# Moving one low-part subtraction ahead of the layer-norm block in GpSimd's loop (gated cross-attention block, one Trainium2 core)

## The chip, the cores and the metric

The kernel runs on one core of one Trainium2 chip. The metric is the device time of one execution in microseconds. Three executions of the kernel before took 1097.84, 1102.97 and 1105.66 us; the median is 1102.97 us.

## The reference, cut to what matters

x and ctx are 128 batches of 128 rows by 256 columns in float32; there are 16 heads of 16 columns. The mask is one 128 by 128 pattern for all batches.

```python
def reference(x, ctx, mask, g_xattn, g_ffn, Wv, bv, Wk, bk, Wq, bq, Wo, bo, W1, W2, W3, b):
    q = layernorm(x) @ Wq + bq
    k, v = ctx @ Wk + bk, ctx @ Wv + bv
    energy = einsum('nqhd,nkhd->nhqk', q, k)        # by head
    energy = where(mask == 0, finfo.min, energy)
    attn = softmax(energy / sqrt(16))
    x = x + tanh(g_xattn) * (einsum('nhqk,nkhd->nqhd', attn, v) @ Wo + bo)
    h = layernorm(x) @ W1 @ W2 @ W3
    return x + tanh(g_ffn) * tanh(h + b)
```

## The kernel before, in words

The 128 batches are taken in pairs: `NP` is 64 pairs, and every engine has a loop over `t` from 0 to 63 with its own order written out by hand. Nothing schedules the work but this order and semaphores. Several stages of different pairs are in flight in one iteration: scores and softmax of pair t, projections of pair t+1, the layer norm of x of pair t+2, the transport of the attention result of pair t-2, its division and output projection for pairs t-3 and t-4, the second layer norm of pair t-4, and the feed-forward part of pairs t-5 and t-6. One iteration is called a period here.

Float32 products of full accuracy are made from two parts: a tile is split into a high part (ScalarE copies it into the float32r type, line 748) and a low part (the tile less its high part: line 958 on VectorE, lines 414 and 425 on GpSimd). A projection (`project`, line 503, `project_T`, line 496) then takes 12 matmuls.

The attention result of a pair, `a_den`, leaves as sums and denominators. SyncE writes it to DRAM (`write_a`, line 263), reads the denominators (`read_den`, 271), writes their reciprocals (`write_reciprocals`, 253), reads the sums in another layout (`read_a`, 277: `a_rows`) and reads the reciprocals spread over the rows (`read_wide`, 258: `den_wide`). GpSimd multiplies both (`divide_a`, line 420: `a_norm`) once both have landed. ScalarE makes the high part of `aT` (`high_of_a`, line 748), GpSimd the low part (`low_of_a`, line 425, which waits for `aT_high` and for the output projection of the pair before). TensorE's output projection of that pair (`make_o`, line 503) comes in the next period. VectorE adds the residual (`add_residual`, 1015) and makes the moments of the second layer norm (`moments_of_y`, 1022 and 1026).

In a period GpSimd works in this order (lines 449 to 473): `low_of_ctx` (414), `add_ffn_bias` (431), `divide_a` (420), `finish` (436), `add_out_bias` (410), a wait for the moments of x of pair t+2 and of y of pair t-4, `rstd` (lines 369 to 383, eight small operations for both), `normalise_x` (389: `xn`), `normalise_y` (389: `yn`), `low_of_a` (425).

TensorE transposes `xn` in `turn_x` (line 490), which waits for `xn_ready` and for `k_ready`: the transposes go to the bank that held the k projection, and ScalarE has to have copied it out (`spread_k`, 773). ScalarE's loop puts `high_of_a` ahead of `spread_q` (773), a softmax exponent (798), `keep_a` (805), `high_of_y` (748) and `spread_k`.

SyncE issues all DMAs of the loop in one order (lines 309 to 332). Its relevant part is `write_reciprocals`, `read_a`, `write_y` (293: `yn` to DRAM, waits for `yn_ready`), `read_max` (288: the row maxima into `q_aug`, for the transposed scores on line 624), `read_wide` (258), then of the next period `store` (305) and `read_y` (299: waits until the write of `yn` has landed), `write_max` (281), `read_den`, `read_max`, `write_a`, the loads of x (202) and ctx (211), `write_max`, and so on to the next `read_a`.

Of the kernel before, what the change touches and what calls it, by code (L numbers as in the profile page):

```python
# [30 lines left out]
def gated_xattn_block(nc, x, ctx, mask, g_xattn, g_ffn, Wv, bv, Wk, bk, Wq, bq, Wo, bo,  # L31
# [9 lines left out]
    with ExitStack() as stack:  # L41
# [123 lines left out]
        def wait(eng, semaphore, value):  # L165
            if value > 0:
                eng.wait_ge(semaphore, value)

        def is_pair(p):
            return 0 <= p < NP  # L170
# [14 lines left out]
        def flat(a):  # L185
            return a.rearrange("p a b -> p (a b)")
# [169 lines left out]
        def _(pool):  # L356
# [7 lines left out]
            def rstd(run):  # L364

                vp, r, a, b, nm = (ln_t[:, j, :] for j in range(5))
                moments = stat2[run % 2][:].rearrange("p a b z -> p (a b) z")
                mean, var = moments[:, :, 0], moments[:, :, 1]
                nc.gpsimd.tensor_tensor(vp, var, c_eps[:], ALU.add).then_inc(ln_step, 1)
                pool.wait_ge(ln_step, RSTD * run + 1)  # L370
                nc.gpsimd.tensor_tensor(r, vp, c_minus_half[:], ALU.pow).then_inc(ln_step, 1)
                pool.wait_ge(ln_step, RSTD * run + 2)
                nc.gpsimd.tensor_tensor(a, r, r, ALU.mult).then_inc(ln_step, 1)
                pool.wait_ge(ln_step, RSTD * run + 3)
                nc.gpsimd.tensor_tensor(b, a, vp, ALU.mult).then_inc(ln_step, 1)
                pool.wait_ge(ln_step, RSTD * run + 4)
                nc.gpsimd.tensor_scalar(a, b, -0.5, 1.5, ALU.mult, ALU.add).then_inc(ln_step, 1)
                pool.wait_ge(ln_step, RSTD * run + 5)
                nc.gpsimd.tensor_tensor(r, r, a, ALU.mult).then_inc(ln_step, 1)
                pool.wait_ge(ln_step, RSTD * run + 6)  # L380
                nc.gpsimd.tensor_tensor(a, mean, r, ALU.mult).then_inc(ln_step, 1)
                pool.wait_ge(ln_step, RSTD * run + 7)
                nc.gpsimd.tensor_scalar(nm, a, -1.0, None, ALU.mult).then_inc(ln_step, 1)  # L383
                pool.wait_ge(ln_step, RSTD * run + 8)
# [7 lines left out]
            def normalise_x(p):  # L392
                wait(pool, xT_done, p)
                pool.wait_ge(x_landed[p % X_RING], 16 * (p // X_RING + 1))
                normalise(0, xn, x_in[p % X_RING], xn_ready)

            def normalise_y(p):
                if p <= END + 1:
                    wait(pool, yn_stored, 16 * p)
                else:  # L400
                    pool.wait_ge(yT_done, p - 1 - END)
                pool.wait_ge(y_ready, p + 1)
                normalise(1, yn, y[p % Y_RING], yn_ready)

            def add_out_bias(p):
                if p == 0:
                    pool.wait_ge(bo_ready, 1)
                pool.wait_ge(xn_ready, PAIR * (p + 1))
                tile = x_in[p % X_RING][:]
                nc.gpsimd.tensor_tensor(tile, tile, bo_wide[:].unsqueeze(1).to_broadcast([P, PAIR, E]), ALU.add).then_inc(x_biased, 1)  # L410

            def low_of_ctx(p):
                pool.wait_ge(cT_high, p + 1)
                nc.gpsimd.tensor_tensor(flat(cT[:, 1]), flat(ctx_T[:]), flat(cT[:, 0]), ALU.subtract).then_inc(cT_ready, 1)

            def divide_a(p):
                pool.wait_ge(a_landed, 16 * (p + 1))
                pool.wait_ge(wide_landed, 16 * (p + 1))
                wait(pool, aT_ready, p)
                nc.gpsimd.tensor_tensor(a_norm[:], a_rows[:], den_wide[:], ALU.mult).then_inc(a_norm_ready, 1)  # L420

            def low_of_a(p):
                pool.wait_ge(aT_high, p + 1)
                wait(pool, o_done, p)
                nc.gpsimd.tensor_tensor(flat(aT[:, 1]), a_norm[:], flat(aT[:, 0]), ALU.subtract).then_inc(aT_ready, 1)

            def add_ffn_bias(p):
                if p == 0:
                    pool.wait_ge(bf_landed, 16)
                pool.wait_ge(f_kept, p + 1)  # L430
                nc.gpsimd.tensor_tensor(th[:], th[:], bf_wide[:].unsqueeze(1).to_broadcast([P, PAIR, E]), ALU.add).then_inc(f_biased, 1)

            def finish(p):
                pool.wait_ge(th_gated, p + 1)
                tile = flat(y[p % Y_RING][:])
                nc.gpsimd.tensor_tensor(tile, tile, flat(th[:]), ALU.add).then_inc(res_ready, 1)
# [12 lines left out]
            for t in range(NP):  # L449
                if t > 0 and is_pair(t + 1):  # L450
                    low_of_ctx(t + 1)
                if is_pair(t - 6):
                    add_ffn_bias(t - 6)
                if is_pair(t - 3):
                    divide_a(t - 3)
                if is_pair(t - 6):
                    finish(t - 6)
                if is_pair(t - 2):
                    add_out_bias(t - 2)
                if t == NP - 1:  # L460
                    add_out_bias(t - 1)
                    add_out_bias(t)
                if is_pair(t + 2):
                    pool.wait_ge(stat1_ready, t + 3)
                if is_pair(t - 4):
                    pool.wait_ge(stat2_ready, t - 3)
                rstd(t + 2)
                if is_pair(t + 2):
                    normalise_x(t + 2)
                if is_pair(t - 4):  # L470
                    normalise_y(t - 4)
                if is_pair(t - 3):
                    low_of_a(t - 3)
            for p in range(NP - 4, NP - 1):
                pool.wait_ge(stat2_ready, p + 1)
                rstd(p + 6)
# [723 lines left out]
```

## Time and profile before

| what | value |
|---|---|
| median of three executions | 1102.97 us (1097.84 to 1105.66) |
| the profiled execution | 1105.66 us |
| its span, first to last instruction | 1103.9 us |
| outside the span | 1.8 us |
| mean granted TensorE clock | 0.987 |
| TensorE busy | 1038.0 us, 94% |
| VectorE busy | 954.7 us, 86% |
| ScalarE busy | 831.2 us, 75% |
| GpSimd busy | 798.3 us, 72% |

The profile gives the busy time of each engine as a share of the span. An engine that is idle is not thereby harmless: it can be idle because it waits in a circle with others. A matmul's end is modelled, so that TensorE's busy time shows only roughly how full it is.

### The profile page before, as it was taken

What the parts mean: (1) busy time and instruction counts of PE and PEld (TensorE: products, weight loads), DVE (VectorE), ACT (ScalarE), POOL (GpSimd) and SP (SyncE); (2) the same over time, 40 slices, a digit from 0 to 9 for tenths busy, and PEclk for the clock granted to TensorE, in tenths of its full rate; (3) what the DMA queues carried; (4) which work ended last, traced back from release to release, by engine and by line L of the source; (5) the groups of instructions that cost most, each with busy time, mean ns of one, the idle gap of its engine ahead of it and who ended that gap; (6) DMA issues with size and microseconds to landing.
All of it is one profiled execution on the core that took longest, in us unless ns stands there. A gap on an engine that the chain in (4) does not pass through costs nothing.

```text
span 1103.9 us, 45278 instructions
## 1 busy us (share of the span) xinstructions
PE 1038.0 (94%) x18487; PEld 897.8 (81%) x18487; DVE 954.7 (86%) x1331; ACT 831.2 (75%) x1275; POOL 798.3 (72%) x1184
## 2 busy tenths in 40 slices
PE   5888999999999999999999999999999999989965
PEld 5777888888888888888888888888788888878855
DVE  5778899889889989889998998999898898888866
ACT  4465878888788787777878878787787877878742
POOL 5254777787787778777778777877777877777653
PEclk9899999999999999999999999999999999999988
DMA  5133555555555564555555556555555555554432
GB/s 150 44 101 104 153 149 159 158 146 155 152 155 155 140 172 139 160 155 146 163 147 154 156 144 168 152 156 149 151 156 145 161 149 154 159 140 138 126 124 68
DMA packets 260400, 158.87 MB, mean 144 GB/s; under 512 B 174945, under 2 KB 227170, under 8 KB 260194
## 3 DMA queue, kind: packets, MB, share of 16 engines
q1 hardware_dynamic: 260050, 155.72, 50.8%
q8 instruction: 147, 2.41, 0.9%
q14 instruction: 59, 0.48, 0.2%
q10 hardware_dynamic: 144, 0.26, 0.1%
HBM read 85.92 MB, written 68.94 MB: 140 GB/s over the span
## 4 chain that ended last, share of the span: by engine, by line
PE 26%; POOL 18%; issue 16%; DMA 15%; SPq 13%; DVE 6%; ACT 6%; POOLq 0%; DVEq 0%; ACTq 0%
PE ps_m L503 6%; DMA a_rows<-scratch_a 5%; PE ps_m L496 5%; PE ps_s L603 4%; PE ps_x L635 3%; DMA scratch_y<-yn 3%; DMA den_wide<-scratch_r 3%; ACT k_aug L773 3%; POOL a_norm L420 3%; SPq L211 3%; SPq L288 3%; POOL yn L389 3%; DVE probs L1007 3%; SPq L299 3%; PE ps_s L624 3%
## 5 line engine op out<-in xcount | busy, mean ns | idle before, releaser
L996 DVE TENSOR_REDUCE neg_max<-ps_s 128x16 f32<-128x2048 f32 x128 | 293.1, 2290 | 68.7 <-PE ps_s L609 68.7
L1007 DVE TENSOR_TENSOR probs<-ps_s,far_T 128x2048 f32<-128x2048 f32 x128 | 291.2, 2275 | 26.3 <-PE ps_s L624 25.5
L798 ACT ACTIVATE probs<-probs 128x2048 f32<-128x2048 f32 x128 | 244.5, 1910 | 5.6 <-DVE probs L1007 5.5
L420 POOL TENSOR_TENSOR a_norm<-a_rows,den_wide 128x512 f32<-128x512 f32 x61 | 78.6, 1288 | 173.6 <-issue 171.6
L603 PE MATMUL ps_s<-k_aug,q_aug 32*128 32x128 f32 x4096 | 150.2, 282 | 17.7 <-DVE probs L1007 7.5
L624 PE MATMUL ps_s<-q_aug,k_aug 32*128 32x128 f32 x4096 | 153.0, 285 | 7.4 <-DMA q_aug<-scratch_m 4.3
L603 PEld LDWEIGHTS ps_s<-k_aug,q_aug 32*128 32x128 f32 x4096 | 127.8, 186 | 38.3 <-issue 30.8
L624 PEld LDWEIGHTS ps_s<-q_aug,k_aug 32*128 32x128 f32 x4096 | 128.7, 188 | 25.4 <-DMA q_aug<-scratch_m 5.8
L635 PE MATMUL ps_x<-probs,v_ones 128*32 128x128 f32 x4096 | 141.2, 279 | 3.9 <-issue 3.1
L773 ACT ACTIVATE q_aug<-ps_m,q_bias,q_scale 128x256 f32<-128x256 f32 x256 | 122.8, 559 | 17.3 <-PE ps_m L496 9.0
L635 PEld LDWEIGHTS ps_x<-probs,v_ones 128*32 128x32 f32 x4096 | 106.1, 111 | 33.5 <-issue 33.4
L773 ACT ACTIVATE k_aug<-ps_m,k_bias,parity 128x256 f32<-128x256 f32 x256 | 123.7, 569 | 11.6 <-PE ps_m L496 10.8
L748 ACT ACTIVATE aT<-a_norm 128x512 fp32r<-128x512 f32 x64 | 40.5, 632 | 114.6 <-POOL a_norm L420 106.1
L565 PE MATMUL ps_m<-wv_s,cT 128*128 128x256 f32 x756 | 118.5, 293 | 0.0
L503 PE MATMUL ps_m<-wo_s,aT 128*128 128x256 f32 x768 | 110.8, 294 | 4.3 <-DVE aT L958 3.1
L496 PE MATMUL ps_m<-cT,wk_s 128*128 128x256 f32 x768 | 109.1, 292 | 3.4 <-DVE wk_s L929 2.0
L503 PEld LDWEIGHTS ps_m<-wo_s,aT 128*128 128x128 f32 x768 | 97.3, 192 | 17.8 <-issue 17.2
L503 PE MATMUL ps_m<-wf_s,yT 128*128 128x256 f32 x756 | 107.1, 292 | 2.8 <-DVE yT L958 2.7
L496 PEld LDWEIGHTS ps_m<-cT,wk_s 128*128 128x128 f32 x768 | 96.1, 190 | 15.9 <-issue 13.2
L496 PE MATMUL ps_m<-xT,wq_s 128*128 128x256 f32 x768 | 108.1, 290 | 0.3 <-DVE xT L958 0.3
L565 PEld LDWEIGHTS ps_m<-wv_s,cT 128*128 128x128 f32 x756 | 99.2, 190 | 8.5 <-issue 1.0
L389 POOL TENSOR_SCALAR xn<-x_in,ln_t 128x256 f32<-128x256 f32 x128 | 97.4, 766 | 6.8 <-POOL ln_t L383 0.2
(123 smaller groups left out, 1769.2 us busy)
## 6 DMA issues: line engine op xcount, KB each, us to landing
scratch_a<-a_den SPq DMA_DIRECT2D x64, 512.0 KB, 3.3
x_in<-in_x SPq DMA_DIRECT2D x64, 256.0 KB, 4.4
a_rows<-scratch_a SPq DMA_DIRECT2D x64, 256.0 KB
den_wide<-scratch_r SPq DMA_DIRECT2D x64, 256.0 KB
out<-y SPq DMA_DIRECT2D x64, 256.0 KB, 4.6
ctx_in<-in_ctx SPq DMA_DIRECT2D x252, 64.0 KB, 2.9
scratch_y<-yn SPq DMA_DIRECT2D x59, 256.0 KB, 3.8
y_blocks<-scratch_y SPq DMA_DIRECT2D x236, 64.0 KB
```

The lines of the kernel that those rows point to most:

```text
L389: nc.gpsimd.tensor_scalar(dst[:, i, :], src[:, i, :], ln_t[:, 1, j:j + 1], ln_t[:, 4, j:j + 1], ALU.mult, ALU.add).then_inc(ready, 1)
L420: nc.gpsimd.tensor_tensor(a_norm[:], a_rows[:], den_wide[:], ALU.mult).then_inc(a_norm_ready, 1)
L496: last = nc.tensor.matmul(dst[:, m * TOK:(m + 1) * TOK], w[:, a, k, m * P:(m + 1) * P], src[:, b, k, :], start=(n == 0), stop=(n == len(TE ...
L503: last = nc.tensor.matmul(dst[:, i * E:(i + 1) * E], src[:, a, k, i * P:(i + 1) * P], w[:, b, k, :], start=(n == 0), stop=(n == len(TERMS) ...
L565: last = nc.tensor.matmul(dst[:, i * E:(i + 1) * E], cT[:, a, k, i * P:(i + 1) * P], wv_s[:, b, k, :], start=(n == 0), stop=(n == len(TERM ...
L603: nc.tensor.matmul(ps_s[:, j, s, :], q_aug[p % 2][rows, n, s, :], k_aug[p % 2][rows, n, s, :], start=(s == 0), stop=False, tile_position=( ...
L624: last = nc.tensor.matmul(ps_s[:, j, s, :], k_aug[p % 2][rows, n, s, :], q_aug[p % 2][rows, n, s, :], start=True, stop=True, tile_position ...
L635: last = nc.tensor.matmul(ps_x[j * ROWS:(j + 1) * ROWS, s, :], v_ones[p % V_RING][:, n, h, :], probs[i % 2][:, j, s, :], start=True, stop= ...
L773: last = nc.scalar.activation(dst[:, :, 2 * m + a, :], src[:, m * TOK:(m + 1) * TOK].rearrange("p (n q) -> p n q", q=P), ACT.Identity, bia ...
L798: nc.scalar.activation(tile, tile, ACT.Exp).then_inc(probs_ready, 1)
L996: nc.vector.tensor_reduce(neg_max[:, 0:H].rearrange("p (j c) -> p j c", j=G), ps_s[:], AX.X, ALU.max, negate=True).then_inc(max_ready, 1)
L1007: nc.vector.tensor_tensor(probs[i % 2][:].rearrange("p j s q -> p (j s) q"), ps_s[:].rearrange("p j s q -> p (j s) q"), far_T[:].unsqueeze ...
```

## The change

On GpSimd, in every period, `low_of_a(t - 3)` is issued after `add_out_bias` and before the wait for the moments, `rstd`, `normalise_x` and `normalise_y`; before, it was the last operation of the period. Its own waits and operands stay as they are. No instruction is added or taken away, and the other engines' orders, SyncE's DMA order among them, are the same.

```diff
@@ -460,6 +460,8 @@
                 if t == NP - 1:
                     add_out_bias(t - 1)
                     add_out_bias(t)
+                if is_pair(t - 3):
+                    low_of_a(t - 3)
                 if is_pair(t + 2):
                     pool.wait_ge(stat1_ready, t + 3)
                 if is_pair(t - 4):
@@ -469,8 +471,6 @@
                     normalise_x(t + 2)
                 if is_pair(t - 4):
                     normalise_y(t - 4)
-                if is_pair(t - 3):
-                    low_of_a(t - 3)
```

GpSimd's order in the middle of a period, before, from the bias on the residual input to the low part of `aT`:

```order
L410 TENSOR_TENSOR x_in<-x_in,bo_wide 128x512
L369 TENSOR_TENSOR ln_t<-stat,c_eps 128x4
L371 TENSOR_TENSOR ln_t<-ln_t,c_minus_half 128x4
L373 TENSOR_TENSOR ln_t<-ln_t 128x4
L375 TENSOR_TENSOR ln_t<-ln_t 128x4
L377 TENSOR_SCALAR ln_t<-ln_t 128x4
L379 TENSOR_TENSOR ln_t<-ln_t 128x4
L381 TENSOR_TENSOR ln_t<-stat,ln_t 128x4
L383 TENSOR_SCALAR ln_t<-ln_t 128x4
L389 TENSOR_SCALAR xn<-x_in,ln_t 128x256 x2
L389 TENSOR_SCALAR yn<-y,ln_t 128x256 x2
L425 TENSOR_TENSOR aT<-a_norm,aT 128x512
```

The same place after the change:

```order
L410 TENSOR_TENSOR x_in<-x_in,bo_wide 128x512
L425 TENSOR_TENSOR aT<-a_norm,aT 128x512
L369 TENSOR_TENSOR ln_t<-stat,c_eps 128x4
L371 TENSOR_TENSOR ln_t<-ln_t,c_minus_half 128x4
L373 TENSOR_TENSOR ln_t<-ln_t 128x4
L375 TENSOR_TENSOR ln_t<-ln_t 128x4
L377 TENSOR_SCALAR ln_t<-ln_t 128x4
L379 TENSOR_TENSOR ln_t<-ln_t 128x4
L381 TENSOR_TENSOR ln_t<-stat,ln_t 128x4
L383 TENSOR_SCALAR ln_t<-ln_t 128x4
L389 TENSOR_SCALAR xn<-x_in,ln_t 128x256 x2
L389 TENSOR_SCALAR yn<-y,ln_t 128x256 x2
```

The subtraction on line 425 now stands ahead of the ten operations that lead to `xn` and `yn`, and these come one operation later; what follows them (line 414, then 431 and 420) directly follows `yn`.

The last iteration, t = 63, which has no `xn` and three biases in a row (line 410, x3), before:

```order
L420 TENSOR_TENSOR a_norm<-a_rows,den_wide 128x512
L436 TENSOR_TENSOR y<-y,th 128x512
L410 TENSOR_TENSOR x_in<-x_in,bo_wide 128x512 x3
L369 TENSOR_TENSOR ln_t<-stat,c_eps 128x4
L371 TENSOR_TENSOR ln_t<-ln_t,c_minus_half 128x4
L373 TENSOR_TENSOR ln_t<-ln_t 128x4
L375 TENSOR_TENSOR ln_t<-ln_t 128x4
L377 TENSOR_SCALAR ln_t<-ln_t 128x4
L379 TENSOR_TENSOR ln_t<-ln_t 128x4
L381 TENSOR_TENSOR ln_t<-stat,ln_t 128x4
L389 TENSOR_SCALAR yn<-y,ln_t 128x256 x2
L425 TENSOR_TENSOR aT<-a_norm,aT 128x512
```

Here too the row of line 425 moves up to stand directly behind the three biases. Pairs 61 to 63 have their low part made on VectorE, which the change does not touch.

## Rows read from the trace of the kernel before

**Rows 1.** The page: busy time and share of the span.
```profile
PE 1038.0 (94%) x18487; PEld 897.8 (81%) x18487; DVE 954.7 (86%) x1331; ACT 831.2 (75%) x1275; POOL 798.3 (72%) x1184
```

**Rows 2.** The page: the chain that ended last, by engine.
```profile
PE 26%; POOL 18%; issue 16%; DMA 15%; SPq 13%; DVE 6%; ACT 6%; POOLq 0%; DVEq 0%; ACTq 0%
```

**Rows 3.** Timeline of TensorE, transposes of xn: start, duration, what [idle before <-releaser].
```profile
504.85 0.66 PE L490 MATMUL ps_m<-ident,xn 128*128 128x128 f32 x4
521.68 0.66 PE L490 MATMUL ps_m<-ident,xn 128*128 128x128 f32 x4 [0.57 <-ACT k_aug L773]
537.71 0.66 PE L490 MATMUL ps_m<-ident,xn 128*128 128x128 f32 x4
```

**Rows 4.** Line 420 alone: duration min/median/max, first and last start.
```profile
L420 POOL TENSOR_TENSOR a_norm<-a_rows,den_wide x61: 1267/1289/1299, 73.8 to 1050.1; 128x512 f32<-128x512 f32 x61
```

**Rows 5.** Timeline of GpSimd over one period.
```profile
513.17 1.29 POOL L420 TENSOR_TENSOR a_norm<-a_rows,den_wide 128x512 f32<-128x512 f32 x1 [3.87 <-issue]
...
516.90 0.20 POOL L369 TENSOR_TENSOR ln_t<-stat,c_eps 128x4 f32<-128x4 f32 x1
...
520.05 1.45 POOL L389 TENSOR_SCALAR xn<-x_in,ln_t 128x256 f32<-128x256 f32 x2
521.49 1.09 POOL L389 TENSOR_SCALAR yn<-y,ln_t 128x256 f32<-128x256 f32 x2
522.54 1.29 POOL L425 TENSOR_TENSOR aT<-a_norm,aT 128x512 fp32r<-128x512 f32 x1
523.78 1.28 POOL L414 TENSOR_TENSOR cT<-ctx_T,cT 128x512 fp32r<-128x512 f32 x1
525.01 1.28 POOL L431 TENSOR_TENSOR th<-th,bf_wide 128x512 f32<-128x512 f32 x1
528.36 1.29 POOL L420 TENSOR_TENSOR a_norm<-a_rows,den_wide 128x512 f32<-128x512 f32 x1 [2.06 <-issue]
```

**Rows 6.** Timeline of SyncE's queue, the two places around read_a.
```profile
506.04 0.41 SPq L293 DMA_DIRECT2D scratch_y<-yn  x1
...
521.26 0.61 SPq L277 DMA_DIRECT2D a_rows<-scratch_a  x1
522.60 0.38 SPq L293 DMA_DIRECT2D scratch_y<-yn  x1
523.03 1.09 SPq L288 DMA_DIRECT2D q_aug<-scratch_m  x2
524.23 0.61 SPq L258 DMA_DIRECT2D den_wide<-scratch_r  x1
```

**Rows 7.** Waits of the whole run: us in total, times, longest.
```profile
POOL a_norm L420 <- issue: 171.6, 60, 5.4
...
POOL ln_t L369 <- DVE stat L1026: 19.8, 16, 7.3
...
SPq L293 <- POOL yn L389: 36.3, 46, 2.5
```

**Rows 8.** Timeline of SyncE's queue: read_wide in two other periods.
```profile
588.34 0.61 SPq L258 DMA_DIRECT2D den_wide<-scratch_r  x1
...
928.42 0.61 SPq L258 DMA_DIRECT2D den_wide<-scratch_r  x1
```

**Rows 9.** Timeline of GpSimd in those periods and the one after.
```profile
585.60 1.09 POOL L389 TENSOR_SCALAR yn<-y,ln_t 128x256 f32<-128x256 f32 x2
592.34 1.27 POOL L420 TENSOR_TENSOR a_norm<-a_rows,den_wide 128x512 f32<-128x512 f32 x1 [1.93 <-issue]
597.48 0.20 POOL L369 TENSOR_TENSOR ln_t<-stat,c_eps 128x4 f32<-128x4 f32 x1 [1.37 <-DVE stat L1026]
602.30 1.08 POOL L389 TENSOR_SCALAR yn<-y,ln_t 128x256 f32<-128x256 f32 x2
609.92 1.29 POOL L420 TENSOR_TENSOR a_norm<-a_rows,den_wide 128x512 f32<-128x512 f32 x1 [2.73 <-issue]
...
933.65 1.30 POOL L420 TENSOR_TENSOR a_norm<-a_rows,den_wide 128x512 f32<-128x512 f32 x1 [3.17 <-issue]
```

**Rows 10.** Timeline of VectorE: the low part of yT.
```profile
519.84 0.69 DVE L958 TENSOR_TENSOR yT<-y_T,yT 128x512 fp32r<-128x512 f32 x1 [0.38 <-ACT yT L748]
```

**Rows 11.** Timelines at the end of the loop: GpSimd, then TensorE.
```profile
1060.78 1.27 POOL L425 TENSOR_TENSOR aT<-a_norm,aT 128x512 fp32r<-128x512 f32 x1
...
1064.88 1.70 PE L503 MATMUL ps_m<-wo_s,aT 128*128 128x256 f32 x12 [0.34 <-DVE th L1049]
```

## The prediction

> **What bounds the kernel now.** I read the page first. Its busy shares [rows 1] show TensorE at 94% and GpSimd at 72%, so at first sight an order on GpSimd cannot matter. The chain that ended last says otherwise [rows 2]: TensorE holds only 26% of it, GpSimd 18%, DMA 15%, SyncE's queue 13%, and 16% is time that nothing in the profile explains. A chain through four engines that repeats is a circle, so I looked for its round time.
>
> The timeline of TensorE gives one side. Its transposes of xn start at 504.85, 521.68 and 537.71 [rows 3]: 16.83 us with 0.57 us of idle time, then 16.03 us with none shown. So TensorE alone could do a period in about 16.04 us. The real mean comes from line 420, whose 61 executions start from 73.8 to 1050.1 [rows 4]: 976.3/60 = 16.27 us. TensorE loses some 0.2 us a period, always at turn_x.
>
> The timeline of GpSimd gives the other side. From the start of a_norm (513.17) to the end of yn (521.49+1.09 = 522.58) are 9.41 us without a gap [rows 5]. I call it the GpSimd leg. From there to the next a_norm (528.36) are 5.78 us, the return leg. In it SyncE sends yn out at 522.60, 0.02 us after it is ready, then the maxima, then den_wide at 524.23, which is issued at 524.84 [rows 6]; a_norm starts 3.52 us after that. GpSimd's own work in the return leg ends at 526.29 and it waits 2.06 us [rows 5]. Over the run it waits 171.6 us in 60 waits ahead of a_norm, 2.86 us each, and SyncE waits for yn in 46 periods [rows 7]. So in most periods this holds: a_norm, yn, SyncE's write_y, read_wide, landing, a_norm. GpSimd's idle time is not slack, it is the return leg of a circle that passes through GpSimd itself. The mean return leg is the 3.71 us of work (522.58 to 526.29) and 2.86 us of waiting, 6.57 us, which leaves 16.27-6.57 = 9.70 us for the GpSimd leg: 9.41 and some waits for the moments (19.8 us in 16 waits [rows 7]) and for a longer xn. The circle closes in the same 16.27 us as TensorE's period. Both are bounds within a quarter of a microsecond.
>
> **The change, part by part.** low_of_a leaves the return leg and enters the GpSimd leg. Its price is the distance between starts, 522.54 to 523.78, 1.24 us [rows 5].
>
> In the return leg it was covered: GpSimd waited 2.06 us (mean 2.86) behind it, and what ends the wait is a landing and not GpSimd. Taking it out saves nothing; the wait becomes 1.24 us longer.
>
> In the GpSimd leg it is not covered in full periods: 9.41+1.24 = 10.65 us. Only where GpSimd waits for the moments does it fill that wait, in 16 periods of about 60. It brings no wait of its own: ScalarE's high part is made as soon as a_norm is there, 1.3 us after its start, and low_of_a would come 3.73 us after it (516.90 [rows 5]). Behind it stand rstd, xn and yn. turn_x started 0.18 us after the end of xn at 521.68 (520.05+1.45 = 521.50 [rows 3, 5]), so TensorE gets xn up to 1.1 us late, and SyncE sends yn, the maxima and den_wide 1.24 us late.
>
> What is gained by the early aT is nothing: TensorE reads it a period later. In the last iteration the low part ends at 1062.05 and the projection starts at 1064.88, released by a bias on VectorE [rows 11], so the end gains nothing either.
>
> The return leg after the change is the unknown. It is 0.02 us, then 1.63 us from write_y to the issue of den_wide, 0.61 us for that issue [rows 6] (2.26 us together), and the landing. The landing depends on what shares the DMA engines, most of all a_rows, issued just ahead of yn. If yn comes later, a_rows has had more of them to itself. The nearest rows are the 16 of 55 periods in which den_wide was issued at least 2.6 us behind the end of read_a's issue. Their landings run from 3.39 us (588.95 to 592.34) to 4.62 us (929.03 to 933.65) [rows 8, 9], with a mean of 3.91. The new return leg is then 2.26+3.9, about 6.15 us, and between 5.65 and 6.9. The new period is 10.65+6.15 = 16.8 us, with 16.3 and 17.5 as ends.
>
> A second circle checks this. From write_y (506.04) over all of SyncE's period to the end of read_a's issue (521.87) are 15.83 us, and from there 6.49 us to a_norm (528.36) [rows 5, 6]; with the new GpSimd leg two periods take 15.83+6.49+10.65 = 32.97, 16.5 us each. I take the middle of 16.5 and 16.8 with a little more weight on the direct sum, 16.75. Against 16.27 that is 0.5 us for each of the 57 steps from t=4 to t=61 in which the circle exists: 28 us. Below nothing is possible only down to TensorE's 16.04, since no circle can be quicker than it.
>
> The sum: the profiled execution has 1103.9 us of span and 1.8 us around it, 1105.7; with 28 us it would take 1134. The median is 2.7 us below that execution, so the median forecast is 1103+28 = 1131 us.
>
> **A rule beside a row.** The pair of xn took 1.45 us and the equal pair of yn 1.09 [rows 5]. VectorE's subtraction for yT ran from 519.84 to 520.53, across the start of xn at 520.05 [rows 10]. The Trainium skill (SBUF — State Buffer, "SBUF: two separate sides") says that VectorE, in an operation with two SBUF inputs, and GpSimd lock one shared pair of ports against each other for a whole instruction. By that rule the trace agrees, and xn, which moves 1.24 us later, would miss that operation. But VectorE's subtraction then falls on the small operations of rstd, which read SBUF too. I count no gain; the rule's other outcome is the second rival.
>
> **The rivals.**
>
> First, the later issue is paid back by the landing. With den_wide landing at the shortest row, 3.39 us, in all periods, the return leg is 5.65 us and the period 16.3; some periods still hide low_of_a in the wait for the moments. The cost is then 0.03 to 0.15 us a period, about 6 us: 1109. For it speaks that a late issue has short landings (3.52 and 3.39 in rows 6 and 9); against it that 4.62 stands in the same group. The Trainium skill (DMA: Bandwidth & Descriptors, "Latency and other measured facts") says that a lighter memory load makes the fixed part of a DMA smaller, which would help this rival; no row here separates that part.
>
> Second, the change is faster. xn gets rid of the collision with yT's subtraction (0.36 us, 1.45 less 1.09), and rstd doesn't pick it up. The GpSimd leg is 10.29 us, and with 5.65 the circle closes in 15.94 us, less than TensorE's 16.04. Then TensorE never waits and the period is 16.04: 57 times 0.23 is 13 us less, 1090. It decides only if both hold, and the shortest of 55 landings would have to be the rule. Very unlikely.
>
> Third, it is worse than forecast. When yn was late in the kernel before, the return leg did not shorten. In the period with a_norm at 592.34 GpSimd waited 1.37 us for the moments, yn ended at 603.38, and the next a_norm came at 609.92, 6.54 us later [rows 9]. A return leg of 6.45 with 10.65 is 17.1 us, 0.85 more than now: 48 us, 1151. For it speaks that SyncE's later reads (yn's blocks, the maxima of both halves) shift as well, and TensorE can wait for maxima where it waited for xn. Against it: that period's a_norm had come early, so part of the distance is TensorE's own time.
>
> **How the numbers follow.** The forecast, 1131 with 1117 to 1145 around it, has 0.66. The first rival (1109) has 0.17, the second (1090) 0.05, the third (1151) 0.12. A difference under about 1%, 11 us, can't be told from none in this kernel. Slower by over 1% is the forecast and the third rival, 0.78; within 1% is the first, 0.17; faster is the second, 0.05. The range takes in the first rival and the third and leaves out the second: 1106 to 1152.
>
> **What would show it.** In the trace after, a_norm's starts should lie 16.75 us apart on average. From a_norm to the end of yn should be 10.6 to 10.7 us, and waits for the moments rare. turn_x should start 0.18 us or less after the end of xn in nearly every period, with TensorE idle some 0.6 us ahead of it. SyncE should wait longer ahead of write_y than 36.3/46 = 0.8 us, and the wait ahead of a_norm should be more than 2.86 us. ScalarE's wait for a_norm should not be what TensorE then waits for. If a_norm's distance stays at 16.3 with a GpSimd leg of 10.65, the first rival was right, and den_wide's landing shows it; if the leg itself is under 10.4, the collision is gone. The prediction is wrong if TensorE's idle time doesn't grow at turn_x, or if another operation than a_norm, yn or xn is what it waits for.

## The result, and the profile after

The changed kernel takes 1151.9 us (median of four executions, 1150.81 to 1156.32 us) against 1103.03 us for the kernel before. The ratio is 1.0446, with a 95% interval of 1.0416 to 1.0478: 4.5% slower, 49 us. The profiled execution has a span of 1145.9 us, 42.0 us more than the 1103.9 us of before. The profiled execution of before was the slowest of its kernel (1105.66 us, 2.6 us above the median), that of the changed kernel the fastest of its (1147.69 us, 4.2 us below the median); so the profiles show 42 us and the medians 49.

The page of the changed kernel, busy shares and the chain that ended last, by engine:

```profile
PE 1032.0 (90%) x18487; PEld 894.1 (78%) x18487; DVE 954.2 (83%) x1331; ACT 831.6 (73%) x1275; POOL 797.5 (70%) x1184
...
POOL 42%; issue 27%; DMA 10%; SPq 9%; PE 7%; DVE 5%; POOLq 0%; ACT 0%; DVEq 0%
```

No engine has more to do than in [rows 1] (ScalarE's 0.4 us more is nothing in 831). What changed is the chain: TensorE's share of it fell from 26% in [rows 2] to 7%, and GpSimd's rose from 18% to 42%, at a busy share of 70%. That fits a circle through GpSimd that closes in every period.

Line 420 alone (duration min/median/max, first and last start):

```profile
L420 POOL TENSOR_TENSOR a_norm<-a_rows,den_wide x61: 1267/1289/1301, 73.8 to 1089.4; 128x512 f32<-128x512 f32 x61
```

The mean distance is (1089.4-73.8)/60 = 16.93 us, where [rows 4] gave 16.27. The 60 steps account for 39.3 of the 42.0 us.

The timeline of GpSimd over a full period of the changed kernel (start, duration, what; idle time before it and its releaser in brackets), the rows that answer to [rows 5]:

```profile
512.94 1.29 POOL L420 TENSOR_TENSOR a_norm<-a_rows,den_wide 128x512 f32<-128x512 f32 x1 [2.72 <-issue]
...
516.68 1.28 POOL L425 TENSOR_TENSOR aT<-a_norm,aT 128x512 fp32r<-128x512 f32 x1
517.93 0.19 POOL L369 TENSOR_TENSOR ln_t<-stat,c_eps 128x4 f32<-128x4 f32 x1
518.20 1.04 POOL L371 TENSOR_TENSOR ln_t<-ln_t,c_minus_half 128x4 f32<-128x4 f32 x1
519.32 0.20 POOL L373 TENSOR_TENSOR ln_t<-ln_t 128x4 f32<-128x4 f32 x1
519.60 0.20 POOL L375 TENSOR_TENSOR ln_t<-ln_t 128x4 f32<-128x4 f32 x1
519.89 0.73 POOL L377 TENSOR_SCALAR ln_t<-ln_t 128x4 f32<-128x4 f32 x1
...
521.61 1.09 POOL L389 TENSOR_SCALAR xn<-x_in,ln_t 128x256 f32<-128x256 f32 x2
522.68 1.09 POOL L389 TENSOR_SCALAR yn<-y,ln_t 128x256 f32<-128x256 f32 x2
524.77 1.28 POOL L414 TENSOR_TENSOR cT<-ctx_T,cT 128x512 fp32r<-128x512 f32 x1 [1.00 <-ACT cT L748]
526.00 1.29 POOL L431 TENSOR_TENSOR th<-th,bf_wide 128x512 f32<-128x512 f32 x1
529.80 1.29 POOL L420 TENSOR_TENSOR a_norm<-a_rows,den_wide 128x512 f32<-128x512 f32 x1 [2.50 <-issue]
```

The leg from a_norm to the end of yn is 523.77-512.94 = 10.83 us here, and the return leg 529.80-523.77 = 6.03 us, together 16.86. GpSimd now waits twice in the return leg, for the high part of cT (1.00 us) and for the landing (2.50 us). Both lie in the shadow of SyncE's path: GpSimd could do more work there, but the leg would not get shorter with less. The same place in SyncE's queue and on TensorE:

```profile
521.44 0.61 SPq L277 DMA_DIRECT2D a_rows<-scratch_a  x1
523.80 0.38 SPq L293 DMA_DIRECT2D scratch_y<-yn  x1
524.23 1.09 SPq L288 DMA_DIRECT2D q_aug<-scratch_m  x2
525.42 0.60 SPq L258 DMA_DIRECT2D den_wide<-scratch_r  x1
```

```profile
522.85 0.63 PE L490 MATMUL ps_m<-ident,xn 128*128 128x128 f32 x4 [1.18 <-POOL xn L389]
539.63 0.63 PE L490 MATMUL ps_m<-ident,xn 128*128 128x128 f32 x4 [0.90 <-POOL xn L389]
```

write_y leaves 0.03 us behind yn, den_wide is issued at 526.02, and a_norm starts 3.78 us later. TensorE starts its transposes 0.15 us behind the end of xn (522.70) and stood idle for 1.18 and 0.90 us; in [rows 3] that was 0.57 us and nothing.

The waits of the whole run (us in total, times, longest):

```profile
POOL a_norm L420 <- issue: 163.6, 60, 3.8
...
POOL cT L414 <- ACT cT L748: 85.2, 62, 11.8
...
PE ps_m L490 <- POOL xn L389: 62.8, 58, 1.5
...
SPq L293 <- POOL yn L389: 96.4, 59, 2.4
```

SyncE waits for yn in all 59 periods in which there is a write_y, 1.63 us each, where [rows 7] had 46 waits of 0.8 us. TensorE waits for xn 58 times, 1.08 us each.

The whole run can be split in the same way. Each period in which there is a write_y runs from one a_norm to the next; the trace has 59 of them. In microseconds:

| mean of 59 periods | before | forecast | after |
|---|---|---|---|
| GpSimd leg, a_norm to the end of yn | 9.65 | 10.65 | 10.73 |
| return leg, end of yn to the next a_norm | 6.63 | 6.15 | 6.24 |
| period | 16.29 | 16.80, taken as 16.75 | 16.98 |

write_y leaves within 0.1 us of the end of yn in 50 of these periods before and in all 59 after. The landing marks in the trace (the semaphore updates of each DMA) show which transfer GpSimd waits for: in both kernels a_norm starts 0.12 to 0.41 us after the last mark of den_wide, and never less than 2.2 us after the last mark of a_rows.

### The profile page after: what moved, and what is told of

Same layout as the page of the kernel before. It is cut to its first block, busy times and chain, and to the rows that moved or that the text cites. A ratio compares the mean times of both kernels' runs of the same rounds, so it can differ in the third digit from the quotient of the medians.

```text
span 1145.9 us, 45278 instructions
## 1 busy us (share of the span) xinstructions
PE 1032.0 (90%) x18487; PEld 894.1 (78%) x18487; DVE 954.2 (83%) x1331; ACT 831.6 (73%) x1275; POOL 797.5 (70%) x1184
## 3 DMA queue, kind: packets, MB, share of 16 engines
q8 instruction: 147, 2.41, 0.9%
## 4 chain that ended last, share of the span: by engine, by line
POOL 42%; issue 27%; DMA 10%; SPq 9%; PE 7%; DVE 5%; POOLq 0%; ACT 0%; DVEq 0%
DMA den_wide<-scratch_r 9%; POOL y L436 6%; POOL xn L389 5%; POOL aT L425 5%; POOL yn L389 5%; POOL ln_t L371 5%; SPq L288 5%; POOL x_in L410 5%; POOL ln_t L377 3%; SPq L293 2%; DVE probs L1007 2%; POOL ln_t L379 2%; DVE neg_max L996 2%; PE ps_s L603 1%; PE ps_s L624 1%
## 5 line engine op out<-in xcount | busy, mean ns | idle before, releaser
L996 DVE TENSOR_REDUCE neg_max<-ps_s 128x16 f32<-128x2048 f32 x128 | 293.2, 2291 | 71.2 <-PE ps_s L609 71.2
L420 POOL TENSOR_TENSOR a_norm<-a_rows,den_wide 128x512 f32<-128x512 f32 x61 | 78.6, 1289 | 167.1 <-issue 163.6
L635 PE MATMUL ps_x<-probs,v_ones 128*32 128x128 f32 x4096 | 138.9, 276 | 2.8 <-issue 2.0
L414 POOL TENSOR_TENSOR cT<-ctx_T,cT 128x512 fp32r<-128x512 f32 x62 | 79.1, 1276 | 85.2 <-ACT cT L748 85.2
L748 ACT ACTIVATE xT<-ps_m 128x512 fp32r<-128x512 f32 x65 | 38.9, 598 | 105.9 <-PE ps_m L490 103.3
```

What stands on the lines that cost most here:

```text
L635: last = nc.tensor.matmul(ps_x[j * ROWS:(j + 1) * ROWS, s, :], v_ones[p % V_RING][:, n, h, :], probs[i % 2][:, j, s, :], start=True, stop= ...
L748: nc.scalar.activation(flat(dst[:, 0]), src, ACT.Copy).then_inc(ready, 1)
L996: nc.vector.tensor_reduce(neg_max[:, 0:H].rearrange("p (j c) -> p j c", j=G), ps_s[:], AX.X, ALU.max, negate=True).then_inc(max_ready, 1)
```

## The experiments

Each ran beside the kernel before on the same chip; the median of the latter was 1099.31 us for the first four, 1098.08 us for the next four and 1097.73 us for the last two. Ratios are against that, in the order of the text. The period is the mean distance of a_norm's 61 starts. Its first and last start are given with each.

**Which of the two late tiles costs: xn or yn.** The low part stands between them, so xn is on time and yn is not.

```diff
                 if is_pair(t + 2):
                     normalise_x(t + 2)
+                if is_pair(t - 3):
+                    low_of_a(t - 3)
                 if is_pair(t - 4):
                     normalise_y(t - 4)
-                if is_pair(t - 3):
-                    low_of_a(t - 3)
```

> The subtraction of line 425 stands between xn and yn: xn is as early after a_norm as before, only yn is 1.24 us later. Circle theory (a_norm, yn, SyncE's write_y and read_wide, landing, a_norm sets the period): the leg from a_norm to the end of yn is 10.65 to 10.75 us, the return 6.2, period 16.9 to 17.0, about 1145 to 1152 us like the changed kernel, and TensorE no longer waits for xn but for k_aug. Rival, that TensorE gets xn late and this alone costs: 1103 us as before. A time between (about 1125) would mean that both count.

It took 1143.21 us, ratio 1.0405 (1.037 to 1.0439). The period is (1084.8-71.4)/60 = 16.89 us, against 16.93 in the changed kernel. GpSimd and TensorE in one of its periods:

```profile
512.11 1.29 POOL L420 TENSOR_TENSOR a_norm<-a_rows,den_wide 128x512 f32<-128x512 f32 x1 [3.95 <-issue]
...
519.00 1.45 POOL L389 TENSOR_SCALAR xn<-x_in,ln_t 128x256 f32<-128x256 f32 x2
520.42 1.29 POOL L425 TENSOR_TENSOR aT<-a_norm,aT 128x512 fp32r<-128x512 f32 x1
521.69 1.10 POOL L389 TENSOR_SCALAR yn<-y,ln_t 128x256 f32<-128x256 f32 x2
529.20 1.28 POOL L420 TENSOR_TENSOR a_norm<-a_rows,den_wide 128x512 f32<-128x512 f32 x1 [3.93 <-issue]
```

```profile
520.63 0.65 PE L490 MATMUL ps_m<-ident,xn 128*128 128x128 f32 x4 [1.03 <-ACT k_aug L773]
```

xn ends 8.34 us behind a_norm, as in [rows 5], and TensorE now waits for k_aug and not for xn, yet almost the whole cost is there (4.05 of 4.46%). The lateness of yn alone makes it. That TensorE waited for xn in the changed kernel is then a symptom: something has to be late for it once the circle is longer than its own period, and what is named changes with the order.

**Is it the low part itself, or the length of the leg?** The changed kernel, with `add_out_bias` moved behind yn in exchange.

```diff
-                if is_pair(t - 2):
-                    add_out_bias(t - 2)
...
                 if is_pair(t - 4):
                     normalise_y(t - 4)
+                if is_pair(t - 2):
+                    add_out_bias(t - 2)
```

(The biases of the last two pairs at t = 63 move along.)

> The changed kernel (low part early), but add_out_bias goes behind yn in exchange: the leg has as many operations as before. Circle theory: only the length of the leg counts, 9.4 to 9.6 us, and the time is that of before, 1103 us give or take 4. Rival, that the early low part itself hurts (its place beside VectorE's and the DMAs' work): 1140 us or more stay.

It took 1098.29 us, ratio 0.9972 (0.9951 to 0.9992), period (1035.0-71.2)/60 = 16.06 us (in the fastest of its ten executions, 1091.83 us). The low part is as early as in the changed kernel and costs nothing. What counts is how much work stands in the leg.

**Can the leg be made shorter than before?** The order before, with the bias behind the low part (the same move as above on the order before).

> The order before, with add_out_bias moved from ahead of the moments' wait to behind the low part of aT. Circle theory: the leg is 9.41 less 1.24, about 8.2 us, the circle closes in 14.4 us or less than TensorE's 16.04, so TensorE's own period shows: about 1090 us (57 x 0.23 = 13 us less than before). Rival, xn's lateness alone: before the change xn was on time, so nothing is gained, 1103 us. Rival, SyncE's own round (15.83 us and more) or the moments' wait takes over: 1097 to 1103 us.

It took 1098.64 us, ratio 0.9995 (0.9973 to 1.0016), period 16.12 us: no gain, a miss of the circle theory's 1090. The waits say why:

```profile
POOL a_norm L420 <- issue: 92.9, 60, 3.1
POOL ln_t L369 <- DVE stat L1026: 89.2, 62, 8.9
```

GpSimd now waits for the moments in every period, 1.44 us each: the time taken out of the leg became a wait for VectorE's moments, and the leg is on average as long as before (9.65 us). In the kernel before two limits lie close together, as the prediction said, and to shorten one of them gains nothing. TensorE's transposes come in a median distance of 16.04 us already in the kernel before, and in e3 and e4 too; what the kernel before had above that in the profiled execution is small, and that execution was the slowest of its kernel.

**The dose.** A second subtraction of the same size, to a spare tile that nothing reads, ahead of the low part: once in the changed kernel (in the leg), once in the kernel before (in the return leg). The output is not touched.

```diff
+                nc.gpsimd.tensor_tensor(spare[:], a_norm[:], flat(aT[:, 0]), ALU.subtract)
                 nc.gpsimd.tensor_tensor(flat(aT[:, 1]), a_norm[:], flat(aT[:, 0]), ALU.subtract).then_inc(aT_ready, 1)
```

> The changed kernel with a second subtraction of the same size (to a spare tile that nothing reads) beside the low part, so the leg is 1.24 us longer once more. Circle theory: the circle is closed in every period by now, so the full price is paid: 57 x 1.24 = 71 us more than the changed kernel, 1222 us. Rival, that the price of an operation in the leg is the same each time (49 us as for the first): 1201 us. Rival, TensorE or DMA bound after the change: under 1165 us.

> The order before, with a second subtraction of 1.24 us (to a spare tile that nothing reads) beside the low part behind yn, so in the return leg. Circle theory: the return is set by SyncE's queue and the landing, GpSimd waits 2.9 us in it on average, and the operation costs nothing: the time of before, within 1%. Rival, that GpSimd's total work counts: at least 20 us more, 71 at the full price of 57 x 1.24. A cost of a few us would come from periods with a landing so short that GpSimd's wait is under 1.24 us.

In the return leg it cost nothing: 1098.2 us, ratio 0.9999 (0.9979 to 1.0018). GpSimd's wait ahead of a_norm shrank from 171.6 us in [rows 7] to 90.1 us. So 1.24 us more work for GpSimd per period is free there, and GpSimd's total is not what decides.

In the leg it cost 1202.27 us, ratio 1.0929 (1.0889 to 1.0969): 103 us over the kernel before, 54 more than the change alone. That is a little above the first dose of 49, so nearest to the rival's 1201, and under the full price of 71 that the circle theory gave. Two periods of line 420 (here 421) and what VectorE does between:

```profile
523.71 1.29 POOL L421 TENSOR_TENSOR a_norm<-a_rows,den_wide 128x512 f32<-128x512 f32 x1 [2.69 <-issue]
...
530.21 1.05 POOL L372 TENSOR_TENSOR ln_t<-ln_t,c_minus_half 128x4 f32<-128x4 f32 x1
...
534.17 1.10 POOL L390 TENSOR_SCALAR yn<-y,ln_t 128x256 f32<-128x256 f32 x2
...
541.53 1.28 POOL L421 TENSOR_TENSOR a_norm<-a_rows,den_wide 128x512 f32<-128x512 f32 x1 [2.41 <-issue]
```

```profile
530.74 0.63 DVE L960 TENSOR_TENSOR yT<-y_T,yT 128x512 fp32r<-128x512 f32 x1
```

The leg is 535.27-523.71 = 11.56 us and not 10.83+1.24 = 12.07. VectorE's subtraction for yT falls on the power operation, which takes 1.05 us as always; in the changed kernel it fell on a small one, which took 0.73 us in place of 0.20. The half microsecond between is that collision. The return leg is 6.26 us.

Over the run this closes the sum. VectorE's subtraction began while the power operation ran in 40 periods. The six small operations on lines 373 to 383 (374 to 384 here) took 95.9 us in all, against 111.3 in the changed kernel: 15 us less. The full price of 1.24 us in 59 periods is 73 us, less 15 is 58, and the two profiled executions differ by 58.2. So the leg is paid at the full price, and the shortfall is the collision. What TensorE's clock added is small (last section).

**The way back, in SyncE's order.** First the changed kernel with den_wide ahead of the maxima:

```diff
                 if is_pair(t - 4) and t - 4 <= END:
                     write_y(t - 4)
-                read_max(2 * t + 1)
                 if is_pair(t - 2):
                     read_wide(t - 2)
+                read_max(2 * t + 1)
```

> The changed kernel, with read_wide issued ahead of read_max(2t+1) in SyncE's order, directly behind write_y: den_wide goes out 1.19 us earlier after yn, the maxima 0.65 us later. Circle theory: return leg 6.22 less 1.19 = 5.03 us, leg 10.75, together 15.8, under TensorE's 16.04: the time comes back to about 1100 us, or up to 1120 if TensorE now waits for the maxima. Rival, that xn's lateness against TensorE costs and SyncE's place doesn't matter: 1149 us or more. Rival, the landing is limited by what shares the DMA engines and grows by what is issued earlier: 1135 to 1149.

It took 1117.26 us, ratio 1.0143 (1.0092 to 1.0195), period (1056.1-72.6)/60 = 16.39 us. Two thirds of the cost (3.0 of 4.5%) are back with no change on GpSimd, which xn's place alone can't explain. Of the rest a part is explained: the maxima are late now. In the 12 periods in which TensorE stood over 0.3 us ahead of line 624 the transposes were 17.11 us apart, in the other 47 it was 16.19; that is 11 us of some 19. What makes up the remainder is not shown; from the issue of den_wide to a_norm it took 4.28 us on average here against 3.97 in the changed kernel, which took back part of what the earlier issue gave. The waits for the maxima, and one of them on TensorE:

```profile
PEld ps_s L624 <- DMA q_aug<-scratch_m: 20.1, 26, 2.4
```

```profile
520.14 1.17 PE L624 MATMUL ps_s<-q_aug,k_aug 32*128 32x128 f32 x32 [1.10 <-DMA q_aug<-scratch_m]
```

Then write_y behind both reads, so that den_wide doesn't wait for yn at all; once in the changed kernel and once in the kernel before:

```diff
-                if is_pair(t - 4) and t - 4 <= END:
-                    write_y(t - 4)
                 read_max(2 * t + 1)
                 if is_pair(t - 2):
                     read_wide(t - 2)
+                if is_pair(t - 4) and t - 4 <= END:
+                    write_y(t - 4)
```

> The changed kernel, with write_y moved behind read_max(2t+1) and read_wide in SyncE's order: den_wide no longer waits for yn, and the circle through a_norm and yn is cut. Circle theory: the period falls from 16.97 us; what is left is SyncE's own round (15.83 us, and up to 1.7 more, since less stands between write_y and the read that waits for its landing) and TensorE's 16.04: 1100 to 1130 us. Rival, that the lateness of xn or yn costs by another way than read_wide: 1149 us or more.

> The kernel before, with the same move in SyncE's order (write_y behind read_max(2t+1) and read_wide). Circle theory: the circle was within a quarter of a microsecond of TensorE's period, so cutting it gives at most the 0.1 to 0.2 us a period that TensorE loses at turn_x, 1090 to 1100 us, unless SyncE's own round takes over, then up to 1125 us and the same time as the changed kernel with this move. If both kernels with this move take the same time, the place of the low part costs only through read_wide.

Both got slower: 1166.54 us, ratio 1.0626 (1.0578 to 1.0674), and 1173.94 us, ratio 1.0681 (1.065 to 1.0712). Both are misses: 1100 to 1130 and at most 1125 us were expected. The rows fit SyncE's own round taking over, with more than I had forecast. Its queue in the first of them:

```profile
502.08 0.40 SPq L293 DMA_DIRECT2D scratch_y<-yn  x1
502.54 0.46 SPq L305 DMA_DIRECT2D out<-y  x1
506.40 1.82 SPq L299 DMA_DIRECT2D y_blocks<-scratch_y  x4
...
518.81 0.41 SPq L293 DMA_DIRECT2D scratch_y<-yn  x1
```

```profile
SPq L299 <- DMA scratch_y<-yn: 191.2, 59, 5.7
```

From write_y to the read that needs its landing are 4.3 us, and only the store stands between; the queue waits 3.24 us in each of 59 periods. The round is 16.73 us here without any wait for yn, and the period of the run is (1105.6-73.5)/60 = 17.20 us. Where the other half microsecond comes from is not shown. What these two runs show is still of use: once den_wide no longer waits for yn, the early low part is no longer the slower order (1.0626 against 1.0681 for the order before). The two differ in the granted clock too (0.986 and 0.971 in the profiled executions), so they don't show that it is the faster one. The maxima and den_wide had stood between write_y and the read that waits for its landing, so to take them away from there was not free.

**The rest of TensorE's loss.** ScalarE's high part of aT behind the query copies, with and without the late bias:

```diff
-                if is_pair(t - 3):
-                    high_of_a(t - 3)
                 if is_pair(t + 1):
                     spread_q(t + 1)
+                if is_pair(t - 3):
+                    high_of_a(t - 3)
```

> The order before with two moves: add_out_bias behind the low part of aT (as in e3), and on ScalarE high_of_a behind spread_q, so that a late a_norm holds back neither the query copies nor what follows them up to k_aug. Circle theory: what TensorE still loses in the kernel before (median period 16.04 us, mean 16.1 to 16.25) comes from periods with a late landing, and reaches it over xn and k_aug, both about 8.4 us behind a_norm. With both paths shortened the mean goes to 16.04: 1090 to 1094 us, 0.5 to 0.8% under the kernel before. Rival, the rest is SyncE's or VectorE's: 1098 us, nothing gained.

> The order before with only ScalarE's move (high_of_a behind spread_q). Circle theory: xn still ends 8.33 us behind a_norm and holds TensorE 0.13 us less than k_aug did, so alone it gains at most 1 us: 1097 to 1099 us. Rival, that ScalarE's wait for a_norm (106 us in 59 waits) is by itself what TensorE loses: 1091 us.

1098.11 us, ratio 0.9993 (0.9976 to 1.001), and 1098.09 us, ratio 1.0007 (0.9984 to 1.003). The first is a miss: there is nothing left to gain here. TensorE's waits for k_aug at turn_x in the kernel before, and in the first of these two:

```profile
PE ps_m L490 <- ACT k_aug L773: 6.7, 14, 1.0
...
PE ps_m L490 <- ACT k_aug L773: 6.3, 37, 0.3
```

The longest wait fell from 1.0 to 0.3 us, but the total was small to begin with, and the time is the same. None of the ten kernels is faster than the kernel before by more than 0.3%.

## Why the prediction was wrong

The direction and the mechanism were right, the size was not: 28 us were forecast, 49 came, and the ratio of 1.0446 puts the time just past the upper end of the range (1.0446 times 1102.97 is 1152.2, and the range ended at 1152). The step that failed is the size of the growth per period, "Against 16.27 that is 0.5 us for each of the 57 steps": it was 0.69 us in 59 steps. By its parts:

- **The circle.** Right. e1 shows that yn's lateness alone makes nearly all of the cost with xn on time, e7 that an earlier den_wide takes two thirds of it back, e6 that the same work is free in the return leg, e4 that an equal operation taken out of the leg pays for the one put in, e5 that a second one is paid at its full price, less a collision.
- **The GpSimd leg, 10.65 us, a growth of 0.95 over 9.70.** The largest part of the miss. It grew by 1.08, from 9.65 to 10.73. The base of the new leg was one period of 9.41 us, whose collision of xn with VectorE's subtraction cost 0.36 us; on average the two legs had 0.45 us of it before and 0.44 after. The waits for the moments, which had lengthened the mean leg of before, did go, as forecast. So 0.08 of the missing 0.13 us is the collision, the rest that the leg before was a little shorter than the 9.70 read for it. 0.13 us in 59 periods is 8 us.
- **The return leg, 6.15 us.** Nearly right: 6.24 on average, 0.39 us shorter than before where 0.42 were forecast. The issue of den_wide to a_norm took 3.97 us on average, where 3.91 stood behind the forecast. The difference is 2 us in the sum.
- **"I take the middle of 16.5 and 16.8 with a little more weight on the direct sum, 16.75."** This took off another 0.05 us, 3 us in all, and it was wrong in kind. The second circle closes over the landing of a_rows, and a_rows had landed at least 2.2 us before a_norm started in every period, before and after. It had room and didn't bind. The longest circle sets the period, not a mean of circles.
- **The base.** The 16.27 us of before are from the slowest execution of its kernel, the 16.93 of after from the fastest of its. The medians lie 2.6 and 4.2 us the other way, and these 7 us are the difference between 42 and 49. A range that comes from one profiled execution of each kernel has to be that much wider.
- **57 steps.** Two too few. SyncE writes yn in 59 periods (t = 4 to 62), which is 1 us.
- **First rival** (the landing pays it back): half right. The landing did pay back some 0.4 us, as the forecast had it too, and not the rest; a_norm's distance grew. **Second** (faster): xn's collision did go, as its first half said, but rstd picked it up. **Third** (1151 us, a period of 17.1): nearest in its number, by luck. Its return leg of 6.45 us stands in no row (the row it points to gives 6.54), the measured one was 6.24, and the legs add up to 16.98 and not 17.1; the rest came with the executions that were profiled. SyncE's late reads did not make TensorE wait for maxima in the changed kernel; that wait appears in e7.
- **What would show it.** As forecast: transposes 0.15 us behind xn, SyncE waiting longer for yn, few waits for the moments (4 against 16). Not as forecast: TensorE's idle time at turn_x was 1.08 us and not 0.6, and the wait ahead of a_norm did not grow (163.6 us against 171.6), because GpSimd now waits earlier in the return leg, for cT's high part (85.2 us), which the low part used to cover.

Where the collision went can be read from the totals of the whole run (line, count, busy time in us and mean of one in ns, idle time before), before:

```profile
L389 POOL TENSOR_SCALAR xn<-x_in,ln_t 128x256 f32<-128x256 f32 x128 | 97.4, 766 | 6.8 <-POOL ln_t L383 0.2
L377 POOL TENSOR_SCALAR ln_t<-ln_t 128x4 f32<-128x4 f32 x69 | 13.9, 201 | 6.4
L379 POOL TENSOR_TENSOR ln_t<-ln_t 128x4 f32<-128x4 f32 x69 | 14.4, 209 | 5.7
```

and after:

```profile
L389 POOL TENSOR_SCALAR xn<-x_in,ln_t 128x256 f32<-128x256 f32 x128 | 71.3, 564 | 6.7
L377 POOL TENSOR_SCALAR ln_t<-ln_t 128x4 f32<-128x4 f32 x69 | 31.5, 456 | 6.4
L379 POOL TENSOR_TENSOR ln_t<-ln_t 128x4 f32<-128x4 f32 x69 | 21.5, 312 | 5.7
```

xn lost 26.1 us, and the two small operations gained 24.7. The change moved the collision and left its size as it was.

## What to carry to other kernels

When an engine's idle time ends with a landing, ask whether the DMA was issued behind something that this same engine makes: then the idle time is one side of a circle, and it matters on which side of the DMA's trigger an operation stands. Add up each circle from rows, over all its periods and not from one. Take the longest and not a mean: a circle whose landing is there long before it is used has room. In this kernel a move of one operation ahead of the trigger was paid back by moving another of equal length behind it.

## What the runs showed of the hardware

Two VectorE inputs from SBUF against a GpSimd operation: nearly every GpSimd operation of xn or rstd that meets VectorE's 0.63 to 0.69 us subtraction for yT gets longer, whichever it is. It was xn in the kernel before (1.45 us for the pair against 1.09) and line 377 in the changed kernel (0.73 against 0.20). The exception is the 1.05 us power operation. Per period the collision cost 0.45 us before, 0.44 after and 0.20 in e5.

The Trainium skill (SBUF — State Buffer, "SBUF: two separate sides") says that whoever starts first holds the shared ports for its whole instruction. By that rule the trace agrees in [rows 10], where VectorE started first and xn was the one to lengthen. By the recorded starts it does not agree where GpSimd was first. In 29 periods of the kernel before, VectorE's subtraction began 0.03 to 0.26 us into a running operation of xn, took its usual 0.63 us, and xn was again the one to lengthen (1.06 to 1.15 us for one that takes 0.55 alone). In the changed kernel line 377 started at 519.89 and VectorE at 519.94. In e5 VectorE's subtraction started 40 times within the power operation, with up to 0.89 us of it left, and neither of the two got longer.

TensorE's granted clock stayed at its upper level (2.4 GHz) through the loop of the changed kernel, in spite of a wait of about 1.1 us for xn in nearly every period. In e5, where the wait was 1.66 us on average, it fell 15 times between 100 and 1140 us to the lower level (0.5 of full clock, 1.2 GHz), for 3.4 us each. Each time a wait for xn of 1.77 to 2.39 us had just ended or was ending, but not every wait of that length was followed by a fall. Around one of them at 534 us in e5 (stretch in us from the span's start; busy times of TensorE, its weight loads, VectorE, ScalarE and GpSimd with their counts; granted clock, DMA share, GB/s), and the matmul groups there and a period earlier:

```profile
516.00:534.00 18.00, 15.78 (x288) 13.69 (x288) 14.91 (x21) 13.03 (x20) 13.64 (x20) 1.00 0.50 138
535.40:538.80 3.40, 3.40 (x41) 3.18 (x39) 1.50 (x5) 2.41 (x4) 2.23 (x2) 0.51 0.47 155
```

```profile
516.96 1.67 PE L505 MATMUL ps_m<-wf_s,yT 128*128 128x256 f32 x12
...
534.34 0.63 PE L492 MATMUL ps_m<-ident,xn 128*128 128x128 f32 x4 [1.87 <-POOL xn L390]
534.72 2.41 PE L505 MATMUL ps_m<-wf_s,yT 128*128 128x256 f32 x12
537.07 1.96 PE L605 MATMUL ps_s<-k_aug,q_aug 32*128 32x128 f32 x32
```

Twelve matmuls took 2.41 us where the same twelve took 1.67 us a period earlier. The cost in e5 is small: the distance of a_norm in the period after a fall was 18.21 us on average, in the periods clear of a fall 17.85, which makes an estimate of at most 5 us in the 15 periods.
